# Turning a pair's top-p flags on TensorE behind both tiles' logits, in the second step of a graph attention kernel

## Chip, cores and metric

One core of a Trainium2 chip runs the whole program, in float32 throughout except for some masks. The metric is the device time of one execution in microseconds (us); less is better. TensorE is PE in the profile, its weight loads PEld, VectorE is DVE, ScalarE is ACT, GpSimd is POOL and the DMA queue's engine is SP.

## The reference, cut to what matters

The input is `x`, 3327 rows by 128, and a sparse 3327 x 3327 matrix `adj`. The first layer makes two steps; each of them builds an attention matrix over all rows, keeps in each row only the largest probabilities that together reach 0.9 (top-p), and multiplies. The second layer (signs of `adj`, three heads, gates) follows and is not touched by the change.

```python
def _top_p_attention(X, W1, W2, W3):
    q = X @ W1.T @ W2.T
    k = X @ W3.T
    logits = q @ k.T / TAU
    probs = jax.nn.softmax(logits, axis=-1)
    idx = jnp.argsort(-probs, axis=-1)
    sp = jnp.take_along_axis(probs, idx, axis=-1)
    cs = jnp.cumsum(sp, axis=-1)
    keep_sorted = cs - sp < TOP_P
    ...
    A = probs * mask
    return A / jnp.maximum(A.sum(-1, keepdims=True), 1e-12)
...
for n in range(STEPS):
    A = _top_p_attention(Xa, W1, W2, W3)
    Xf = R @ Xf
    Xa = A @ Xa
    Z = Z + Xf @ U1[n].T + Xa @ U2[n].T
```

`R` is `adj` plus the identity, each row divided by its sum. `X` and `Xa` are 3327 x 128, `q` and `k` 3327 x 64.

## The kernel before

**Tiles and pairs.** The rows are padded to 26 tiles of 128, worked on as 13 pairs, 0 to 12. A tile's logits are 3327 columns wide: seven chunks of up to 512 (`NC`), for which there are two PSUM banks (`lg`), copied by ACT into the tile's row buffer `e`. There are two sets of `e`, so the logits of pair p + 2 go where pair p was, once pair p has been attended. The function `layer0` holds both steps; five engine programs stand side by side in it, each with a fixed order, tied by semaphores.

**Step two (`step == 1`), the part that changes.** Attention runs for the 13 pairs, and between them TensorE does the two products with `adj` (`rows`): 26 units of one pair of tiles in two hops, each unit two tiles of 1 + 26 matmuls. One turn of each engine, for pair p, in program order:

- TensorE (`pair_with_rows`, L992): `take_rows` (L875) gathers the rows that pair p could not settle; `attend` (L944) for the two tiles turns `e` and multiplies it with the features, the first waiting for `select` of tile 0 of pair p and the second for that of tile 1; then `logits(p + 2, 0)`, `turn_flags(p + 1)`, `logits(p + 2, 1)` (L825 and L857); then a chain of small turns and products that go back and forth with ACT (`update_all_rows` L986, `turn_attended` L948, `update` L955); then `rows` (L829) for four tiles.
- VectorE (`pair_with_rows`, L1372), already one pair further while TensorE works on pair p: `search(p + 1)` (L1303) finds the thresholds and ends with `flags_ready`; `tops` (L1285) of the two tiles of pair p + 2 reads their logits in segments of 64 (L71), each waiting for that tile's seven copied chunks by `lg_free`; `assign_slots(p + 1)` (L1314) waits for `flagT_ready`, the turned flags; then it waits for POOL's marks, and `select` (L1346) of the tiles of pair p + 1 lets TensorE attend them (`w_ready`).
- ACT (L1206) copies out what TensorE leaves in PSUM, and takes the exponentials of pair p + 2 (`exps_of`) between the copies of the `rows` tiles.
- POOL (L751): the queries of pair p + 2 (`give_q`), in the first half the scaling of the rows, then `find_marks(p + 1)` (L740), which waits for the same flags as TensorE, then the sums into `H` (`add_rows` L726, `give_attended` L701).

**Turning the flags** (`turn_flags`, L857) is two transposes of one column each (L861) and two products with four columns that count slots (L863 and L864), into the bank `small`. It waits until VectorE's search of that pair is over:

```python
eng.wait_ge(flags_ready, turn_of(step, p) + 1)
eng.wait_ge(rowA_ready, seq(step, p, 0) + 1)
```

**The loops.** `over_pairs_with_rows` (L640) rolls TensorE's pairs 0 to 3 and 7 to 10 in loops of two pairs and writes out pairs 4, 5, 6, 11 and 12; on VectorE 0 to 5 and 7 to 10 are rolled. Pair 6 has one unit of rows to update, the others two. Logits and flags ahead exist for pairs 0 to 10 (`rest >= 2`); for pair 11 only flags.

Of the kernel before, what the change touches and what calls it, by code (L numbers as in the profile page):

```python
# [518 lines left out]
def layer0(nc, d, dims, H, ident):  # L519
# [15 lines left out]
    with ExitStack() as ctx:  # L535
# [77 lines left out]
        def turn_of(step, p):  # L613
            return p + step * PAIRS
# [12 lines left out]
        def at(p, n):  # L627
            return isinstance(p, int) and p == n

        def units_of(p, hop):  # L630

            if at(p, TURN):
                return [(PAIRS - 1, 0)]
            if hop == 0:
                return [(p * 2, 0), (p * 2 + 1, 1)]
            return [(p * 2 - 1, 1), (p * 2, 0)]
# [19 lines left out]
        with nc.Block() as block:  # L656
# [137 lines left out]
            def _(eng):  # L794
# [6 lines left out]
                for step in range(2):  # L801
# [9 lines left out]
                    def logit(p, k, c):  # L811
                        if c == 0 and at(p, PAIRS):
                            eng.wait_ge(taken_q_ready, 1)
                        elif c == 0:
                            eng.wait_ge(qs_ready, seq(step, p, k) + 1)
                        bank = chunk(step, 0, k, c) % 2
                        sl = cols(c, N)
                        eng.wait_ge(lg_free, chunk(step, p, k, c) + 1)
                        eng.matmul(lg[bank][:, 0:sl.stop - sl.start], qs[k][:, :], kT[:, sl],  # L819
                                   start=True, stop=True).then_inc(lg_ready, 1)  # L820
                        if c == NC - 1:
                            eng.drain()
                            eng.sem_inc(qs_free, 1)

                    def logits(p, k):  # L825
                        for c in range(NC):
                            logit(p, k, c)

                    def rows(u, hop):  # L829

                        xf = XR[0] if hop == 0 else XR[2]
                        for k in range(2):
                            eng.wait_ge(adj_loaded[k], (u + 1) * 16)
                            eng.wait_ge(accR_read, u * 2 + k + 1)
                            eng.matmul(accR[:, :], ident[:, :],
                                       xf[:, bass.ds((u - hop * PAIRS) * 2 + k, 1), :].rearrange("p a n -> p (a n)"),
                                       start=True, stop=False)
                            for j in range(T):
                                mm = eng.matmul(accR[:, :], adj[k][:, j * P:(j + 1) * P], xf[:, j, :],  # L839
                                                start=False, stop=(j == T - 1))  # L840
                            mm.then_inc(accR_ready, 1)
                            eng.drain()
                            eng.sem_inc(adj_free, 1)
# [13 lines left out]
                    def turn_flags(p):  # L857
                        eng.wait_ge(flags_ready, turn_of(step, p) + 1)
                        eng.wait_ge(rowA_ready, seq(step, p, 0) + 1)
                        for k in range(1 if at(p, PAIRS) else 2):  # L860
                            mm = eng.transpose(flagT[:, k, :], find.flags[:, k:k + 1], ident[:, :])  # L861
                        if step == 1 and not at(p, PAIRS):
                            eng.matmul(slots, ones, find.counts[:, 1, :], start=True, stop=False)  # L863
                            mm = eng.matmul(slots, upto, find.counts[:, 0, :], start=False, stop=True)  # L864
                        mm.then_inc(flagT_ready, 1)
# [9 lines left out]
                    def take_rows(p):  # L875

                        eng.wait_ge(slots_ready, p + 1)
                        for k in range(2):
                            mm = eng.matmul(taken, hot[k],
                                            XR[1][:, bass.ds(p * 2 + k, 1), :].rearrange("p a n -> p (a n)"),  # L880
                                            start=False, stop=at(p, PAIRS - 1) and k == 1)
                        mm.then_inc(taken_ready, 1)

                    def project_taken():

                        eng.wait_ge(taken_copied, 1)
                        eng.wait_ge(zsA_ready, turn_of(step, PAIRS - 1) + 1)
                        eng.wait_ge(zsR_ready, LATE[0][0])
                        eng.transpose(xt[:, 0, :], taken_rows[:, 0:P], ident[:, :]).then_inc(taken_turned, 1)
                        eng.wait_ge(taken_T_ready, 1)  # L890
                        eng.matmul(zp[0:DA, 0, :], W1T[:, :], taken_T, start=True, stop=True).then_inc(taken_h1_made, 1)
                        eng.wait_ge(taken_h1_ready, 1)
                        eng.matmul(zp[0:DA, 1, :], W2T[:, :], taken_h1, start=True, stop=True).then_inc(taken_q_made, 1)
# [50 lines left out]
                    def attend(p, b, k):  # L944
                        for c in range(NC + 1):
                            attend_part(p, b, k, c)

                    def turn_attended(p):  # L948
                        eng.wait_ge(rowA_ready, seq(step, p, 1) + 2)
                        eng.wait_ge(zsA_ready, turn_of(step, p) + 1)  # L950
                        for k in range(2):
                            mm = eng.transpose(xt[:, k, :], rowA[k][:, :], ident[:, :])
                        mm.then_inc(xtA_ready, 1)

                    def update(p):  # L955
                        eng.wait_ge(xTA_ready, turn_of(step, p) + 1)
                        for k in range(2):
                            mm = eng.matmul(zp[:, k, :], xT[:, k, :], UT[:, 1, step, :], start=True, stop=True)
                        mm.then_inc(zA_ready, 1)
# [26 lines left out]
                    def update_all_rows(units, hop):  # L986
                        for u, s in units:
                            eng.wait_ge(zsR_ready, u)
                            turn_rows(u, s)
                            update_rows(u, hop)  # L990

                    def pair_with_rows(p, b, rest, hop, next_hop):  # L992
                        take_rows(p)
                        if at(p, PAIRS - 1):
                            project_taken()
                            logits(PAIRS, 0)
                        attend(p, b, 0)
                        attend(p, b, 1)
                        if rest >= 2:
                            logits(p + 2, 0)  # L1000
                        if rest:
                            turn_flags(p + 1)
                        if rest >= 2:
                            logits(p + 2, 1)
                        eng.wait_ge(zsA_ready, turn_of(step, p) + 1)
                        if rest:
                            update_all_rows(units_of(p, hop), hop)
                            eng.wait_ge(zsR_ready, units_of(p, hop)[-1][0] + 1)
                        turn_attended(p)
                        update(p)  # L1010
                        if next_hop == 1:
                            eng.wait_ge(hop_done, PAIRS + 2)
                        if next_hop is not None:
                            for u, s in units_of(p + 1, next_hop):
                                rows(u, next_hop)
# [27 lines left out]
                    if step == 0:  # L1043
                        turn_flags(0)
                        over_pairs(eng, pair, tail=3)
                    else:
                        for u, s in units_of(0, 0):
                            rows(u, 0)
                        turn_flags(0)
                        over_pairs_with_rows(eng, pair_with_rows)  # L1050
                        late_rows()
                        turn_flags(PAIRS)
                        attend(PAIRS, 1, 0)
                        update_taken()
                        place_taken()
# [1287 lines left out]
```

## Time and profile before

| what | value |
|---|---|
| runs (3) | 2786.88, 2792.64, 2792.99 us; median 2792.64 us |
| the profiled execution's own time | 2795.35 us |
| its span (first to last instruction) | 2793.6 us |
| step two's attention with rows | about 577 us to 1490 us of the span |
| mean granted TensorE clock | 0.932 of full |
| busy: PE, PEld, DVE, ACT, POOL | 84%, 71%, 79%, 38%, 5% of the span |
| DMA | 245 MB, mean 88 GB/s |

How to read the rows further down: in a list of waits, a row says which engine and line waited for which other engine and line, the us in total, how often, and the longest. In a timeline, a row is the start in us from the span's start, how long in us, engine, line, operation, output<-inputs, how many instructions were merged, and in brackets the idle time just ahead of it and what ended it; "issue" means that the profile shows no releaser.

### The profile page before, as it was taken

The page shows a single profiled execution, that of the slowest core. Times are in us where ns is not written, and L with a number is a line of the kernel's source. Part 1 is how long each engine was busy: PE and PEld are TensorE (multiplying, and loading weights), DVE is VectorE, ACT ScalarE, POOL GpSimd, SP SyncE. Part 2 cuts the span into 40 slices and gives each one's busy share as a digit, 9 for nine tenths or more (in the row PEclk, how much of TensorE's full clock was granted, in tenths as well). Part 3 has the DMA queues.
Part 4 walks back from the last instruction along what each step waited for, and adds up shares of the span by engine and source line. Part 5 has one row for each costly group of instructions (what it writes and reads, how often), then busy time and mean ns, then how long its engine had stood idle before and what let it go on. Part 6 is the DMA issues. An engine that isn't in the chain of part 4 may idle for free. (4 is left out here: it accounts for less than half of the span.)

```text
span 2793.6 us, 53551 instructions
## 1 busy us (share of the span) xinstructions
PE 2358.4 (84%) x17759; PEld 1987.9 (71%) x17759; DVE 2201.9 (79%) x6636; ACT 1071.5 (38%) x1785; POOL 140.9 (5%) x353
## 2 busy tenths in 40 slices
PE   5899998767888997887886649996999999999985
PEld 1566666445677776776775539995999999999952
DVE  3777777288887889888789867775999999999846
ACT  4566666432333333332333040003434344443423
POOL 0000000101111111000000010000000000000000
PEclk9999999988898998998997869998999999999997
DMA  3000000020222221222220234543333333333320
GB/s 127 2 2 1 1 1 2 1 99 11 90 100 100 99 100 50 100 99 100 99 99 2 99 127 175 217 171 126 111 115 133 116 130 118 129 120 126 99 87 25
DMA packets 57106, 245.00 MB, mean 88 GB/s; under 512 B 6705, under 2 KB 18352, under 8 KB 43120
## 3 DMA queue, kind: packets, MB, share of 16 engines
q1 hardware_dynamic: 56816, 241.94, 24.7%
q8 instruction: 83, 1.36, 0.2%
q14 instruction: 207, 1.70, 0.2%
HBM read 235.10 MB, written 6.82 MB: 87 GB/s over the span
## 5 line engine op out<-in xcount | busy, mean ns | idle before, releaser
L1933 PE MATMUL a_acc<-H,pT 128*128 128x128 f32 x4056 | 548.0, 277 | 11.1 <-ACT a_rows L1965 3.8
L1933 PEld LDWEIGHTS a_acc<-H,pT 128*128 128x128 f32 x4056 | 495.4, 192 | 28.1 <-DVE pT L2067 19.3
L71 DVE MAX8 cand<-e 128x8 f32<-128x64 f32 (+3 forms) x1898 | 302.6, 239 | 129.4 <-issue 129.2
L935 PE MATMUL small<-XR,wT 128*128 128x128 f32 x2756 | 377.2, 283 | 28.8 <-ACT wT L1132 28.1
L819 PE MATMUL lg<-kT,qs 128*128 128x512 f32 (+1 forms) x742 | 350.8, 612 | 47.1 <-ACT e L1076 34.9
L935 PEld LDWEIGHTS small<-XR,wT 128*128 128x128 f32 x2756 | 343.1, 197 | 45.1 <-ACT wT L1132 45.1
L2067 DVE TENSOR_TENSOR pT<-a_tr,a_adjT 128x512 f32<-128x512 f32 (+1 forms) x546 | 316.6, 645 | 22.3 <-PE a_tr L1892 19.2
L839 PE MATMUL accR<-XR,adj 128*128 128x129 f32 x2704 | 322.8, 281 | 0.0
L1892 PE MATMUL a_tr<-ident,prob 128*128 128x128 f32 x2028 | 311.9, 274 | 10.9 <-ACTq L1959 10.9
L839 PEld LDWEIGHTS accR<-XR,adj 128*128 128x128 f32 x2704 | 319.5, 198 | 0.0
L1132 ACT ACTIVATE wT<-tr 128x512 f32<-128x512 f32 (+1 forms) x371 | 206.0, 566 | 268.3 <-PE tr L925 266.4
L2045 DVE CUSTOM_DVE_ANT_0 prob<-a_adj,EB 128x3328 f32<-128x3328 f32 x78 | 282.6, 3623 | 0.0
L819 PEld LDWEIGHTS lg<-kT,qs 128*128 128x128 f32 x742 | 124.4, 200 | 215.3 <-ACT e L1076 161.8
L1076 ACT ACTIVATE e<-lg 128x512 f32<-128x512 f32 (+1 forms) x371 | 206.1, 566 | 178.7 <-PE lg L819 176.8
L925 PE MATMUL tr<-ident,e 128*128 128x128 f32 x1378 | 214.0, 283 | 47.9 <-DVE scalars L1353 41.7
L1892 PEld LDWEIGHTS a_tr<-ident,prob 128*128 128x128 f32 x2028 | 241.7, 142 | 11.1 <-issue 11.1
L1957 ACT ACTIVATE prob<-prob,a_negmax 128x3328 f32<-128x3328 f32 x78 | 238.9, 3063 | 9.1 <-DVE a_negmax L2054 9.1
L925 PEld LDWEIGHTS tr<-ident,e 128*128 128x128 f32 x1378 | 168.4, 146 | 87.6 <-issue 44.3
L1581 PE MATMUL g_sp<-g_adj,H 128*128 128x128 f32 x1352 | 162.6, 283 | 17.1 <-ACTq L1646 17.1
L1581 PEld LDWEIGHTS g_sp<-g_adj,H 128*128 128x128 f32 x1352 | 158.5, 198 | 18.8 <-issue 18.2
L1086 ACT ACTIVATE e<-e,scalars 128x3327 f32<-128x3327 f32 x53 | 162.1, 3060 | 15.9 <-DVE scalars L1417 8.8
L219 DVE SCALAR_TENSOR_TENSOR work<-cand,mid 128x416 f32<-128x416 f32 (+1 forms) x198 | 143.3, 758 | 8.1
(334 smaller groups left out, 2456.6 us busy)
## 6 DMA issues: line engine op xcount, KB each, us to landing
adj<-in_adjT SPq DMA_DIRECT2D x52, 1664.0 KB, 7.2
g_adj<-in_adjT SPq DMA_DIRECT2D x26, 1664.0 KB, 6.9
a_adj<-in_adj SPq DMA_DIRECT2D x26, 1664.0 KB, 6.8
a_adjT<-in_adjT SPq DMA_DIRECT2D x156, 256.0 KB, 3.9
a_adjT<-in_adjT SPq DMA_DIRECT2D x26, 128.0 KB, 4.2
XT<-in_x_t SPq DMA_DIRECT2D x1, 1664.0 KB, 13.5
hT_scratch<-hT SPq DMA_DIRECT2D x1, 1664.0 KB, 12.1
nsT_scratch<-nsT SPq DMA_DIRECT2D x1, 1664.0 KB, 6.2
```

Source lines behind the costliest of these rows:

```text
L71: eng.max(cand[:, n, :], src[:, n * seg:min((n + 1) * seg, width)])
L819: eng.matmul(lg[bank][:, 0:sl.stop - sl.start], qs[k][:, :], kT[:, sl], start=True, stop=True).then_inc(lg_ready, 1)
L839: mm = eng.matmul(accR[:, :], adj[k][:, j * P:(j + 1) * P], xf[:, j, :], start=False, stop=(j == T - 1))
L925: mm = eng.transpose(tr[(k * NC + c) % 2][:, o:o + P], e[b][k][:, j * P:(j + 1) * P], ident[:, :])
L935: mm = eng.matmul(accA[:, :], wT[(k * NC + c - 1) % 2][:, o:o + P], xa[:, j, 0:P], start=(j == 0), stop=(j == T - 1))
L1076: eng.activation(e[b][k][:, sl], lg[chunk(step, 0, k, c) % 2][:, 0:sl.stop - sl.start], ACT.Copy).then_inc(lg_free, 1)
L1581: mm = eng.matmul(sp[k][:, :], H[:, j, :], adj[q][:, j * P:(j + 1) * P], start=(j == 0), stop=(j == T - 1))
L1892: mm = eng.transpose(tr[g % BANKS][:, (j % 4) * P:(j % 4 + 1) * P], prob[order[n][1]][:, j * P:(j + 1) * P], ident[:, :])
L1933: mm = eng.matmul(acc[:, :], pT[g % RING][:, (j % 4) * P:(j % 4 + 1) * P], H[:, j, :], start=(j == 0), stop=(j == T - 1))
L1957: eng.activation(prob[h][:, :], prob[h][:, :], ACT.Exp, bias=negmax[h][:, :], accum_out=den[h][:, :])
L2045: eng.tensor_tensor_reduce(prob[h][:, :], adj[k][:, :], EB[:, h, :], 1.0, -3.0e38, ALU.add, ALU.max, mx[h][:, :])
L2067: eng.tensor_tensor(pT[g % RING][:, 0:width(c)], tr[g % BANKS][:, 0:width(c)], adjT[:, c * 512:c * 512 + width(c)], ALU.mult).then_inc(pT_ ...
```

## The change

In TensorE's program for step two, `turn_flags(p + 1)` is written behind `logits(p + 2, 1)`. Nothing is added or removed, and no other engine's program is touched. Step one, whose TensorE program has its own `pair`, stays as it was.

```diff
@@ -998,10 +998,9 @@
                         attend(p, b, 1)
                         if rest >= 2:
                             logits(p + 2, 0)
+                            logits(p + 2, 1)
                         if rest:
                             turn_flags(p + 1)
-                        if rest >= 2:
-                            logits(p + 2, 1)
                         eng.wait_ge(zsA_ready, turn_of(step, p) + 1)
                         if rest:
                             update_all_rows(units_of(p, hop), hop)
```

**Place 1.** TensorE, the rolled pairs of step two, from the end of `logits(p + 2, 0)`. L819 are the logits, L861 to L864 the flags' turn, L859 the wait for the flags, L818 with `l0_qs_ready` that for the next tile's queries. Before:

```order
L819 MATMUL lg<-kT,qs 128x512 [waits l0_lg_free]
L818 REGISTER_ALU
L819 MATMUL lg<-kT,qs 128x255 [waits l0_lg_free]
L859 ISA [waits l0_flags_ready]
L861 MATMUL small<-ident,pair_flags 1x128 [waits l0_rowA_ready]
L861 MATMUL small<-ident,pair_flags 1x128
L863 MATMUL small<-counts,XT 128x4
L864 MATMUL small<-counts,XT 128x4
L815 REGISTER_ALU
L818 ISA [waits l0_qs_ready]
L819 MATMUL lg<-kT,qs 128x512 [waits l0_lg_free]
```

The same place in the changed kernel:

```order
L819 MATMUL lg<-kT,qs 128x512 [waits l0_lg_free]
L818 REGISTER_ALU
L819 MATMUL lg<-kT,qs 128x255 [waits l0_lg_free]
L815 REGISTER_ALU
L818 ISA [waits l0_qs_ready]
L819 MATMUL lg<-kT,qs 128x512 [waits l0_lg_free]
```

The wait for the flags and the four kinds of flag matmuls are gone from between the tiles; the second tile's first chunk follows the first tile's last.

**Place 2.** TensorE, a few instructions on, at the end of `logits(p + 2, 1)`; L846 and L848 begin the chain of small updates. Before:

```order
L819 MATMUL lg<-kT,qs 128x512 [waits l0_lg_free]
L818 REGISTER_ALU
L819 MATMUL lg<-kT,qs 128x255 [waits l0_lg_free]
L846 ISA [waits l0_zsR_ready,l0_zsA_ready]
L848 MATMUL xz<-ident,rawR 128x128 [waits l0_rowR_ready]
```

In the changed kernel:

```order
L819 MATMUL lg<-kT,qs 128x512 [waits l0_lg_free]
L818 REGISTER_ALU
L819 MATMUL lg<-kT,qs 128x255 [waits l0_lg_free]
L859 ISA [waits l0_flags_ready]
L861 MATMUL small<-ident,pair_flags 1x128 [waits l0_rowA_ready]
L861 MATMUL small<-ident,pair_flags 1x128
L863 MATMUL small<-counts,XT 128x4
L864 MATMUL small<-counts,XT 128x4
L846 ISA [waits l0_zsR_ready,l0_zsA_ready]
L848 MATMUL xz<-ident,rawR 128x128 [waits l0_rowR_ready]
```

The wait for the flags now stands ahead of the updates and of the rows behind them, and no longer ahead of logits.

**Place 3.** VectorE, the end of a search and what follows it, which is the same in both kernels: `tops` of two tiles, each behind the copied logits (`l0_lg_free`), then `assign_slots` at L1318 behind the turned flags.

```order
L1288 ISA
L1290 MEMSET gate 128x1 [waits l0_lg_free]
L71 MAX cand<-e 128x8 x52
L1293 TENSOR_REDUCE scalars<-cand 128x1
L1295 TENSOR_SCALAR scalars<-scalars 128x1
L1288 ISA
L1290 MEMSET gate 128x1 [waits l0_lg_free]
L71 MAX cand<-e 128x8 x52
L1293 TENSOR_REDUCE scalars<-cand 128x1
L1295 TENSOR_SCALAR scalars<-scalars 128x1
L1318 TENSOR_REDUCE pair_flag_top<-small 1x2 [waits l0_flagT_ready]
```

Nothing moved here; what moves are the times at which the second wait for `l0_lg_free` and the wait for `l0_flagT_ready` are met.

## Rows read from the trace of the kernel before

**Rows 1.** The waits of VectorE, then of TensorE, 576 to 1500 us.
```profile
DVE cand L71 <- issue: 34.9, 11, 9.6
...
PE small L861 <- DVEq L326: 46.1, 8, 9.6
```
**Rows 2.** Timeline of TensorE in pair 2, a pair without a wait for flags.
```profile
826.70 0.38 PE L861 MATMUL small<-ident,pair_flags 128*1 128x128 f32 x2 [0.25 <-issue]
...
827.28 6.12 PE L819 MATMUL lg<-kT,qs 128*128 128x512 f32 x14
833.75 0.43 PE L848 MATMUL xz<-ident,rawR 128*128 128x128 f32 x2 [0.35 <-issue]
...
838.71 0.66 PE L952 MATMUL xz<-ident,rowA 128*128 128x128 f32 x2 [0.66 <-ACT zsR L1125]
```
**Rows 3.** Timeline of TensorE in pair 1, which waits for the flags of pair 2.
```profile
748.36 0.59 PE L861 MATMUL small<-ident,pair_flags 128*1 128x128 f32 x2 [5.84 <-DVEq L326]
...
749.45 8.66 PE L819 MATMUL lg<-kT,qs 128*128 128x512 f32 x14
758.37 0.41 PE L848 MATMUL xz<-ident,rawR 128*128 128x128 f32 x2 [0.26 <-issue]
```
**Rows 4.** Timeline of VectorE: its idle times ahead of `tops`, searches 1 to 5 and 7 to 10.
```profile
680.58 0.22 DVE L71 MAX8 cand<-e 128x8 f32<-128x64 f32 x1 [2.48 <-issue]
...
758.58 0.22 DVE L71 MAX8 cand<-e 128x8 f32<-128x64 f32 x1 [2.81 <-issue]
...
826.91 0.22 DVE L71 MAX8 cand<-e 128x8 f32<-128x64 f32 x1 [7.07 <-issue]
...
912.04 0.22 DVE L71 MAX8 cand<-e 128x8 f32<-128x64 f32 x1 [2.95 <-issue]
...
974.10 0.22 DVE L71 MAX8 cand<-e 128x8 f32<-128x64 f32 x1 [0.86 <-issue]
...
1121.46 0.22 DVE L71 MAX8 cand<-e 128x8 f32<-128x64 f32 x1 [1.95 <-issue]
...
1193.45 0.22 DVE L71 MAX8 cand<-e 128x8 f32<-128x64 f32 x1 [1.73 <-issue]
...
1271.17 0.22 DVE L71 MAX8 cand<-e 128x8 f32<-128x64 f32 x1 [2.31 <-issue]
...
1341.34 0.22 DVE L71 MAX8 cand<-e 128x8 f32<-128x64 f32 x1 [9.61 <-issue]
```
**Rows 5.** Timeline of TensorE in pairs 6, 7 and 8: flags' turn and start of updates.
```profile
1112.09 0.59 PE L861 MATMUL small<-ident,pair_flags 128*1 128x128 f32 x2 [7.85 <-DVEq L326]
...
1121.24 0.41 PE L848 MATMUL xz<-ident,rawR 128*128 128x128 f32 x2 [0.29 <-issue]
...
1184.39 0.59 PE L861 MATMUL small<-ident,pair_flags 128*1 128x128 f32 x2 [5.36 <-DVEq L326]
...
1193.27 0.43 PE L848 MATMUL xz<-ident,rawR 128*128 128x128 f32 x2 [0.34 <-issue]
...
1261.45 0.59 PE L861 MATMUL small<-ident,pair_flags 128*1 128x128 f32 x2 [6.09 <-DVEq L326]
...
1271.12 0.41 PE L848 MATMUL xz<-ident,rawR 128*128 128x128 f32 x2 [0.41 <-issue]
```
**Rows 6.** Timeline of TensorE in pair 11, with updates right behind a wait for flags.
```profile
1479.13 0.59 PE L861 MATMUL small<-ident,pair_flags 128*1 128x128 f32 x2 [5.13 <-DVEq L326]
...
1480.22 0.67 PE L848 MATMUL xz<-ident,rawR 128*128 128x128 f32 x2
...
1485.91 0.69 PE L952 MATMUL xz<-ident,rowA 128*128 128x128 f32 x2 [0.47 <-ACT zsR L1125]
```
**Rows 7.** Timeline of TensorE in pair 2: the first two tiles of `rows`.
```profile
841.29 7.10 PE L839 MATMUL accR<-XR,adj 128*128 128x129 f32 x52
...
849.17 5.97 PE L839 MATMUL accR<-XR,adj 128*128 128x129 f32 x52
```
**Rows 8.** Timeline of VectorE in search 3: the second tile's `tops`.
```profile
834.14 6.68 DVE L71 MAX8 cand<-e 128x8 f32<-128x64 f32 x52
```

## The prediction

> **What bounds the kernel now.** I read the waits of step two first [rows 1]. VectorE sits idle ahead of its `tops` (L71) for 34.9 us in 11 pieces; "issue" names no releaser, but L1290 in front of them waits for copied logits and nothing else. TensorE waits 46.1 us for VectorE's flags in 8 pieces (L861 behind the last drain of the search). So the two engines wait for each other in turns, and both waits meet at the place that the change touches. Then the timelines. In pair 2 [rows 2] the flags are ready when TensorE comes: it goes from flags at 826.70 over the second tile's logits at 827.28 to the updates at 833.75, so a tile's logits take 833.75 - 827.28 = 6.47 us. In pair 1 [rows 3] it waits 5.84 us at the flags; then the logits, 6.12 us in pair 2, take 8.66 us, and from flags to updates it is 758.37 - 748.36 = 10.0 us, of which 749.45 - 748.36 = 1.1 us are the flags' turn. VectorE, which has just finished the search, reads the first tile at once, but must wait for the second (2.81 us at 758.58) [rows 4]. These logits depend on nothing of the search: they stand behind the flags by program order alone.
>
> **The change part by part.** No instruction and no DMA is added or removed; two matters move.
>
> *The flags' turn goes behind the second logits.* Where the flags are ready, it comes 6.5 us later. That costs nothing: VectorE needs it at L1318, after the second tile's `tops`, which starts when the same logits are copied and takes 6.68 us [rows 8], against 0.58 us for the turn (827.28 - 826.70) [rows 2]. If that cover were gone, each pair would pay 0.6 to 1.1 us.
>
> *The second logits go ahead of the wait.* I follow how much earlier each engine gets to its work, pair by pair. VectorE's gain is what it no longer waits. TensorE's gain, where a wait for the flags is left, is VectorE's gain at that search plus the time from flags to updates less the 1.1 us of the turn. A wait of w is left if w, plus TensorE's lead over VectorE, exceeds 6.5 us (a logits' length).
>
> - Searches 1 and 2: VectorE's waits for second tiles go, 2.48 + 2.81 = 5.3 us [rows 4].
> - TensorE, pair 1: it has won some 8.6 us in pair 0 (a whole slow second logits, 8.66 us in [rows 3]), VectorE 2.5; 5.84 + 6.1 - 6.5 = 5.4 us of wait are left, so it gains 2.5 + 10.0 - 1.1 = 11.4 us [rows 3].
> - Search 3 waits 7.07 us for the first logits of pair 4, which TensorE made late. TensorE is now ahead by 11.4 - 5.3 = 6.1 us, so 6.1 of the 7.07 go. Searches 4 and 5: 2.95 and 0.86 go [rows 4]. VectorE has gained 5.3 + 6.1 + 3.8 = 15.2 us. In pairs 2 to 5 TensorE doesn't wait for flags any more and is further ahead than that; in pair 6, with one unit of rows for two, it waits for VectorE's `select`, so its lead is lost and both stand at 15.2 us.
> - Pairs 6, 7 and 8 have waits of 7.85, 5.36 and 6.09 us [rows 5], and a wait is left in each (7.85 - 6.5, and more with the lead in the other two). VectorE gains 1.95 (search 7) and 1.73 us (search 8), so 18.9 us at search 9 [rows 4]. TensorE's gain in pair 8 is 18.9 + (1271.12 - 1261.45) - 1.1 = 18.9 + 8.6 = 27.5 us; by the same sum it had 23.2 in pair 6 and 24.9 in pair 7.
> - Pairs 9 and 10 have no wait for flags; TensorE keeps 27.5 us. VectorE gains 2.31 us more in search 9, to 21.2 us, and its 9.61 us of waiting for first logits in search 10 shrink by the 6.3 us between the two. From there both are 27.5 us early, and pairs 11 and 12, the late rows and the second layer follow unchanged.
>
> *What the wait's new place costs.* Behind it stand now the updates. Pair 11, which has no logits to make, shows that pattern already [rows 6]: after 5.13 us of waiting, L848 to L952 take 1485.91 - 1480.22 = 5.69 us, against 838.71 - 833.75 = 4.96 in pair 2 [rows 2]. So 0.73 us in each pair where a wait is left; two of them count in the sum (pair 1, by way of search 3, and pair 8): 1.5 us. The other end is nothing at all, as the updates run partly at half speed in any pair. POOL's marks (`find_marks`) start with the flags and now meet the updates' sums on POOL's queue; in pair 11 they meet likewise, so that is within the 0.73.
>
> The rows show what a wait costs besides itself: after 5.84 us without work the second logits take 8.66 instead of 6.12 us [rows 2, 3], as their first matmuls run at the lower of the two clock levels, 1.2 GHz. The Trainium skill (TensorE: Matmul & The Clock Gate, HAM oscillation) says that a gap in TensorE's work is paid for again by the matmuls behind it, which start slow. The trace agrees. By that rule alone the moved wait would slow `rows` by what it no longer takes from the logits, 2.5 us in each of the two pairs that count, and the gain would be 27.5 - 5.1 = 22.4 us.
>
> The sum: 27.5 - 1.5 = 26.0 us. The profiled execution took 2795.35 us, 2.7 above the median of the runs, 2792.64; so 2769.3 for its like and 2766.6 for the median. The bounds: VectorE's search, `tops` and `select` have no other wait for TensorE worth naming, so the gain can't exceed the 34.9 us of [rows 1]: 2757.7. Below, it is rival A.
>
> **The rivals.**
>
> A. *The lead is not turned into earlier first logits.* Only the waits for second tiles go, 2.48 + 2.81 + 2.95 + 1.95 + 1.73 + 2.31 = 14.2 us, and the 7.07 and 9.61 us stay, because something else paces TensorE: ACT, which takes exponentials between the `rows` copies, or the transfers of `adj`. Against it: TensorE's rows show it busy between the flags of one pair and the next wherever it isn't waiting for VectorE. 2778.4 us.
>
> B. *Nothing.* The second logits turn out to wait as well, for their queries from POOL, or both engines find a new wait (exponentials that come late for the search) as long as the old one. Against it: POOL gives the queries before it waits for the flags itself. 2792 us.
>
> C. *Slower, by the clock.* TensorE now idles just ahead of the updates, which are too sparse to keep it fast, and then of `rows`. After the updates the first tile of rows took 7.10 us, the next 5.97 [rows 7]; about 1.1 us are lost to the lower level today. If the whole first tile ran at half speed, it would cost 5.97 - 1.13 = 4.8 us more in all 11 pairs, 53 us, against 27.5 gained: 2818 us. It decides from 2.5 us more per pair (27.5 / 11). Against it: pair 11 lost 0.73, and only some five pairs keep a wait. The rule of the Trainium skill named above leans this way, but would find no wait left to act on in pairs 2 to 5, 9 and 10.
>
> D. *More.* The slow stretches after the waits go too, and VectorE loses nearly all its 34.9 us: 2760 us.
>
> **How the numbers follow.** A difference below 0.3% (8.4 us) is about what a measurement of this kernel can't tell from none. Forecast (18 to 31 us gained) 0.67; A 0.14; B 0.08; C 0.04; D 0.07. The predicted time is the forecast's, 2766.6. The range takes in D and the bound, less a little for the spread of the runs, down to 2756, and A with some 4 us above it, up to 2782; B and C are left out, 0.12. Faster: 0.67 + 0.14 + 0.07 = 0.88; same 0.08; slower 0.04.
>
> **What would show it.** In the changed profile: waits of L71 in step two down from 34.9 to 5 to 10 us, with none ahead of second tiles. Waits for flags in TensorE (L861) left in five or six pairs, pairs 0, 1, 6, 7, 8 and 11, at 1 to 6 us, about 20 us in all, and none in pair 3. Second logits at 6.1 us everywhere. L848 to L952 at 5.0 to 5.7 us. L1318 never waiting for pairs 1 to 11. Step one and everything from pair 12 on as long as before. I am wrong if TensorE's lead shows up as longer waits for `select` (tr, L925) of the same size, if the waits at first logits stay at 7 and 9.6 us, or if the tiles of `rows` at the lower level grow by more than one per pair.

## The result, and the profile after

The changed kernel takes 2770.14 us in the median of 4 runs (2768.09 to 2773.17), against 2792.81 us for the kernel before in the same job: 22.7 us less, ratio 0.9918, 95% interval 0.9902 to 0.9933. A second job, with 9 runs of it, gave 0.9927 (0.9909 to 0.9945). The prediction was 2766.6 us, with a range of 2756 to 2782. The profiled execution took 2770.99 us against 2795.35, 24.4 us less.

The page of the changed kernel, its span and the rows of TensorE's logits and `rows` matmuls (busy us, mean ns of one, idle ahead and releaser):

```profile
span 2769.2 us, 53551 instructions
...
L819 PE MATMUL lg<-kT,qs 128*128 128x512 f32 (+1 forms) x742 | 339.9, 596 | 50.5 <-ACT e L1075 38.5
...
L839 PE MATMUL accR<-XR,adj 128*128 128x129 f32 x2704 | 327.2, 283 | 0.0
```

The same two rows of the page before:

```profile
L819 PE MATMUL lg<-kT,qs 128*128 128x512 f32 (+1 forms) x742 | 350.8, 612 | 47.1 <-ACT e L1076 34.9
...
L839 PE MATMUL accR<-XR,adj 128*128 128x129 f32 x2704 | 322.8, 281 | 0.0
```

The same instructions are there. The logits are busy 10.9 us less. Before, six second tiles (pairs 0, 1, 3, 6, 7 and 8) took 7.45 to 8.76 us behind a wait for flags, with a granted clock of 0.50 (1.2 GHz) in their first 2 us; now all second tiles take 6.1 us. The `rows` matmuls are busy 4.4 us more.

VectorE's waits in step two, 576 to 1480 us, in the changed kernel (total, times, longest; lines from L1004 on stand one lower than before):

```profile
DVE work L444 <- issue: 28.2, 17, 2.6
...
DVE gate L1304 <- issue: 10.3, 3, 4.7
DVE e L450 <- issue: 6.0, 4, 2.1
DVE cand L71 <- issue: 4.7, 3, 2.9
```

and those rows before that were not shown yet:

```profile
DVE work L444 <- issue: 24.8, 11, 3.3
DVE gate L1305 <- issue: 12.2, 3, 4.4
...
DVE e L450 <- issue: 2.4, 2, 1.3
```

TensorE's waits in the same stretch, changed kernel:

```profile
PE tr L925 <- DVE scalars L1352: 24.6, 4, 11.6
...
PE small L861 <- DVEq L326: 15.0, 8, 3.1
```

VectorE's waits for logits fall from 34.9 us [rows 1] to 4.7, by 30.2 us, and TensorE's for flags from 46.1 to 15.0; part of that comes back as a longer wait for `select` (L925, 16.9 us before). But VectorE's idle times inside `select`, behind its branches (L444 and L450), rise from 27.2 to 34.2 us. A search starts at L1305, in the changed kernel at L1304. The starts of searches 0, 7 and 12, before:

```profile
576.77 0.06 DVE L1305 MEMSET gate<- 128x1 f32 x1
...
1087.62 0.06 DVE L1305 MEMSET gate<- 128x1 f32 x1
...
1454.83 0.06 DVE L1305 MEMSET gate<- 128x1 f32 x1
```

and in the changed kernel, with what is left of the wait in search 10:

```profile
577.99 0.06 DVE L1304 MEMSET gate<- 128x1 f32 x1
...
1078.42 0.06 DVE L1304 MEMSET gate<- 128x1 f32 x1
...
1317.37 0.22 DVE L71 MAX8 cand<-e 128x8 f32<-128x64 f32 x1 [1.59 <-issue]
...
1429.74 0.06 DVE L1304 MEMSET gate<- 128x1 f32 x1
```

From search 0 to search 12 it took 1454.83 - 576.77 = 878.1 us before and 1429.74 - 577.99 = 851.8 after: 26.3 us less. VectorE's waits add up to nearly that: 30.2 for logits, 1.9 at the turns of the loops, less 7.0 in `select`, is 25.1.

Pair 1 on TensorE, changed kernel, timeline:

```profile
737.58 6.13 PE L819 MATMUL lg<-kT,qs 128*128 128x512 f32 x14 [0.39 <-ACT e L1075]
746.37 0.38 PE L861 MATMUL small<-ident,pair_flags 128*1 128x128 f32 x2 [2.66 <-DVEq L326]
...
746.98 0.67 PE L848 MATMUL xz<-ident,rawR 128*128 128x128 f32 x2
...
752.85 0.66 PE L952 MATMUL xz<-ident,rowA 128*128 128x128 f32 x2 [0.66 <-ACT zsR L1124]
...
755.43 6.81 PE L839 MATMUL accR<-XR,adj 128*128 128x129 f32 x52
```

Against [rows 3]: the second logits take 6.13 us, not 8.66; of the wait 2.66 us are left, not 5.84; the updates begin at 746.98, not 758.37. L848 to L952 take 5.87 us, 0.9 more than in a pair without a wait [rows 2] and 1.3 more than in pair 1 before. The first tile of `rows` takes 6.81 us, against 7.44 in pair 1 before; but in pair 8, which keeps a wait too, it takes 7.78 against 6.93.

### The profile page after: what moved, and what is told of

It reads as the page before. It is cut to its first block and busy times, and to the rows that moved or that the text cites. A ratio compares the mean times of both kernels' runs of the same rounds, so it can differ in the third digit from the quotient of the medians.

```text
span 2769.2 us, 53551 instructions
## 1 busy us (share of the span) xinstructions
PE 2355.1 (85%) x17759; PEld 1987.9 (72%) x17759; DVE 2199.7 (79%) x6636; ACT 1072.5 (39%) x1785; POOL 141.5 (5%) x353
## 5 line engine op out<-in xcount | busy, mean ns | idle before, releaser
L1932 PEld LDWEIGHTS a_acc<-H,pT 128*128 128x128 f32 x4056 | 495.3, 192 | 28.7 <-DVE pT L2066 19.9
L935 PE MATMUL small<-XR,wT 128*128 128x128 f32 x2756 | 375.9, 282 | 28.3 <-ACT wT L1131 27.5
L71 DVE MAX8 cand<-e 128x8 f32<-128x64 f32 (+3 forms) x1898 | 302.7, 240 | 101.4 <-issue 101.2
L819 PE MATMUL lg<-kT,qs 128*128 128x512 f32 (+1 forms) x742 | 339.9, 596 | 50.5 <-ACT e L1075 38.5
L2066 DVE TENSOR_TENSOR pT<-a_tr,a_adjT 128x512 f32<-128x512 f32 (+1 forms) x546 | 316.3, 643 | 22.5 <-PE a_tr L1891 19.3
L1891 PE MATMUL a_tr<-ident,prob 128*128 128x128 f32 x2028 | 311.2, 274 | 10.9 <-ACTq L1958 10.9
L819 PEld LDWEIGHTS lg<-kT,qs 128*128 128x128 f32 x742 | 119.0, 193 | 216.9 <-ACT e L1075 168.6
L925 PE MATMUL tr<-ident,e 128*128 128x128 f32 x1378 | 213.2, 282 | 56.0 <-DVE scalars L1352 49.9
L925 PEld LDWEIGHTS tr<-ident,e 128*128 128x128 f32 x1378 | 167.7, 146 | 95.7 <-DVE scalars L1352 51.6
L1580 PEld LDWEIGHTS g_sp<-g_adj,H 128*128 128x128 f32 x1352 | 161.9, 201 | 18.8 <-issue 18.2
```

The source lines that it names most:

```text
L71: eng.max(cand[:, n, :], src[:, n * seg:min((n + 1) * seg, width)])
L925: mm = eng.transpose(tr[(k * NC + c) % 2][:, o:o + P], e[b][k][:, j * P:(j + 1) * P], ident[:, :])
L935: mm = eng.matmul(accA[:, :], wT[(k * NC + c - 1) % 2][:, o:o + P], xa[:, j, 0:P], start=(j == 0), stop=(j == T - 1))
L1580: mm = eng.matmul(sp[k][:, :], H[:, j, :], adj[q][:, j * P:(j + 1) * P], start=(j == 0), stop=(j == T - 1))
L1891: mm = eng.transpose(tr[g % BANKS][:, (j % 4) * P:(j % 4 + 1) * P], prob[order[n][1]][:, j * P:(j + 1) * P], ident[:, :])
L1932: mm = eng.matmul(acc[:, :], pT[g % RING][:, (j % 4) * P:(j % 4 + 1) * P], H[:, j, :], start=(j == 0), stop=(j == T - 1))
```

## Where the extra time in `select` comes from

Search 9's `select` of tile 0 shows both cases. Before, VectorE and SP:

```profile
1281.89 3.62 DVE L439 MATCH_REPLACE8 work<-hits,e 128x3336 f32<-128x3336 f32 x1
1285.58 0.09 DVE L444 MATCH_VALUE_LOAD work<-drops,work 128x8 f32 x1
...
1285.72 14.26 SPq L673 DMA_DIRECT2D adj<-in_adjT  x3
```

In the changed kernel:

```profile
1263.19 14.26 SPq L673 DMA_DIRECT2D adj<-in_adjT  x3
...
1264.27 3.62 DVE L439 MATCH_REPLACE8 work<-hits,e 128x3336 f32<-128x3336 f32 x1
1269.79 0.09 DVE L444 MATCH_VALUE_LOAD work<-drops,work 128x8 f32 x1 [1.91 <-issue]
```

Between L439 and L444 VectorE branches over the rarely run code of another search round. Before, the first transfer of an `adj` tile (three here, some 7 us each) is issued when that branch is already past; now TensorE is further ahead of VectorE, so the transfer is in flight, and VectorE stands idle for 1.91 us. The DMA view of the stretch 1267.5 to 1269.8 us, changed kernel, and of 1285 to 1285.6 us, before (queue, kind: packets, MB, share of 16 engines):

```profile
q1 hardware_dynamic: 58, 0.56, 58.7%
q8 instruction: 1, 0.02, 2.4%
q14 instruction: 1, 0.01, 0.8%
```
```profile
q14 instruction: 1, 0.01, 4.5%
```

A packet of the instruction queue falls into this place in both; before it had the DMA engines to itself and VectorE did not wait.

The timelines of all pairs show the same shift. In `select` of tile 0 the idle at L444 and L450 rises from 3.1 us (2 pieces) to 17.8 (10), as transfers are now under way there; in that of tile 1 it falls from 24.1 to 16.4, as fewer transfers are left by then. The experiments test what the transfers do to it.

## The experiments

Unless said otherwise an edit is made to the changed kernel. Times are medians, ratios those to the kernel before in the same job, with a 95% interval. The runs up to the flags behind the updates were made in one job with the changed kernel's nine runs. The later ones were made in two other jobs, so "less than the changed kernel" compares medians of different jobs there; the kernel before lay between 2792.81 and 2795.38 us in the four jobs. A list of waits comes from one profiled execution.

### The changed kernel again

> The changed kernel once more, so that the other runs of this job have it on their own chip. Both theories: 22 to 26 us below the kernel before, VectorE's waits at L71 in step two 4 to 8 us in all.

2771.29 us in 9 runs (2767.76 to 2781.42), ratio 0.9927. L71 waited 11.9 us in this execution, more than the 4 to 8 expected: search 3 waited 5.45 us for first logits again, and search 10 3.04. L444 and L450 waited 32.1. Single executions differ by some us in how the two engines fall in.

### The new order in one half of the pairs

```diff
                         if rest >= 2:
                             logits(p + 2, 0)
-                            logits(p + 2, 1)
+                            if hop == 0:
+                                logits(p + 2, 1)
                         if rest:
                             turn_flags(p + 1)
+                        if rest >= 2 and not (hop == 0):
+                            logits(p + 2, 1)
```

> The new order in pairs 0 to 6 alone, the old order in pairs 7 to 10. Theory 1 (the gain is VectorE's waits for logits, which TensorE's wait for the flags held up, added up along the chain of pairs): 15 to 17 us faster than the kernel before, and in pairs 7 to 11 L71 waits again, about 15 to 19 us in all. Rival (the gain is the clock: second logits that run slow behind a wait, 2.5 us each, on TensorE's own path): two of the five slow ones are in pairs 0 and 1, so 5 us faster, and VectorE's waits hardly less.

2784.85 us in 10 runs, ratio 0.9971 (0.9955 to 0.9987), so 9.3 us less by the medians and 8 by the ratio. With `hop == 1` in its place, pairs 7 to 10:

> The old order in pairs 0 to 6, the new one in pairs 7 to 10. Theory 1: 8 to 11 us faster than the kernel before; with the run of the first half it adds up to the whole, 24 to 28. Rival (one half frees the path for both): either run alone gives 20 or more, and the sum is well above the whole.

2783.22 us in 10 runs, ratio 0.9971 (0.9957 to 0.9984), 10.9 us less by the medians and 8 by the ratio. VectorE's waits in the first and in the second run:

```profile
DVE work L444 <- issue: 28.0, 16, 3.1
DVE cand L71 <- issue: 21.1, 7, 9.4
```
```profile
DVE cand L71 <- issue: 23.8, 14, 6.6
DVE work L444 <- issue: 19.6, 10, 2.9
```

The second half does what theory 1 said; the first half gives 8 to 9 us, not 15 to 17. Its waits for logits fall by 13.8 us, near the forecast, but a third of that is lost at L444 and L450 (31.6 us against 27.2). Together the two give 16 us by the ratios and 20 by the medians, where the whole gives 20 to 23: not well above it (the rival of the second run falls), and within the intervals not clearly below it, but less than the 24 to 28 of theory 1. The clock rival fails on the waits: it had them hardly less, and in the first half they fell by 13.8 us.

### Flags one step later, behind the updates

```diff
                             logits(p + 2, 0)
                             logits(p + 2, 1)
-                        if rest:
-                            turn_flags(p + 1)
 ...
                         turn_attended(p)
                         update(p)
+                        if rest:
+                            turn_flags(p + 1)
```

> The changed kernel with the flags' turn moved on by one more step, behind the updates and just ahead of the rows. Theory 1: of the 15 us that TensorE still waits for flags nearly all go, but VectorE is what bounds now and has 5 us left to win: 0 to 5 us faster than the changed kernel. Rival (the cover is gone: VectorE's assign_slots, L1317 and after, now waits for the flags' turn, which comes about 8 us after the second logits where tops takes 7): 0.5 to 1 us at L1317 or so in each of 11 pairs, 5 to 11 us slower than the changed kernel.

2781.81 us in 10 runs, ratio 0.9946 (0.9926 to 0.9966): 10.5 us slower than the changed kernel in that job. The size is the rival's; its reason, that the cover is gone, holds in pair 11 alone. In the other pairs something shows that neither had. Timeline near 750 us:

```profile
746.71 0.20 POOL L744 TENSOR_TENSOR pool_gate<-scalars 128x1 f32<-128x1 f32 x1 [23.85 <-DVEq L326]
...
751.15 0.72 POOL L730 TENSOR_TENSOR H<-H,zsR 128x256 f32 x1 [0.35 <-issue]
752.02 0.38 ACT L1124 ACTIVATE zsR<-xz 128x256 f32<-128x256 f32 x1 [4.84 <-POOLq L731]
...
752.64 0.66 PE L952 MATMUL xz<-ident,rowA 128*128 128x128 f32 x2 [4.19 <-ACT zsR L1124]
```

POOL waits for the flags in `find_marks` (L744), and its sums (L730) stand behind that. ACT's copy of the second unit's update needs the first sum, and TensorE's L952 needs the copy. So TensorE waits for the flags by another way: L952 waited 31.9 us in all. And in pair 11, which has no logits, VectorE has no `tops` to cover the turn:

```profile
1467.81 0.41 DVE L1317 TENSOR_REDUCE pair_flag_top<-small 1x2 f32<-1x256 f32 x1 [9.53 <-PE small L864]
```

The starts of the searches tell what each of the two costs. Search 12 of this run:

```profile
1434.07 0.06 DVE L1304 MEMSET gate<- 128x1 f32 x1
```

With search 0 at 578.13 that is 855.9 us for the twelve pairs. The changed kernel took 851.8 in its first profile and 858.1 in the second, so the way by POOL costs no time that shows there, but theory 1's gain isn't there either. From search 12 to the end of the span it takes 1348.7 us, against 1339.5 and 1336.2. So most of the 10.5 us lies behind search 12, where pair 11's wait stands.

To take both away, POOL's marks go behind its sums, and pair 11 stays as in the changed kernel:

```diff
-                            find_marks(p + 1)
+                            if rest == 1:
+                                find_marks(p + 1)
                             for u, s in units_of(p, hop):
                                 add_rows(u, hop)
                             give_attended(p)
+                            if rest >= 2:
+                                find_marks(p + 1)
 ...
```

In TensorE's program `turn_flags` stands behind the updates for `rest >= 2` and where the changed kernel has it for `rest == 1`.

> The run with the flags behind the updates again, with two edits: POOL's find_marks stands behind add_rows and give_attended, and pair 11, which has no logits, keeps flags and marks where the changed kernel has them. Theory (behind updates, TensorE waited for the flags all the same: the second unit's copy on ACT waits for POOL's add_rows, which stands behind find_marks, which waits for the flags; and pair 11 cost VectorE 8 us at L1317): TensorE's waits at L952 fall from 31.9 us to about 9 and no wait of 9.5 us is left at L1317; 8 to 15 us faster than the run behind updates, and 0 to 5 faster than the changed kernel, as VectorE bounds. Rival (TensorE's own late turn holds up VectorE's assign_slots in every pair): waits at L1317 of 5 us or more in all, and no faster than the changed kernel.

2766.75 us in 4 runs, ratio 0.9910 (0.9881 to 0.9938); the runs lie between 2759.04 and 2772.45, and the profiled one is the fastest. VectorE's wait for the turned flags, TensorE's for `select`, at L952 (L955 here) and for the flags:

```profile
DVE pair_flag_top L1322 <- PE small L867: 4.2, 2, 2.9
```
```profile
PE tr L928 <- DVE scalars L1357: 33.4, 9, 12.4
...
PE xz L955 <- ACT zsR L1129: 7.2, 12, 0.7
...
PE small L864 <- DVEq L326: 5.7, 1, 5.7
```

With both mended the loss is gone, and the later turn is as fast as the changed kernel, not measurably faster. Both edits were made in one run, so it doesn't tell them apart; the search starts above put most of the loss on pair 11. TensorE's waits for flags are nearly gone and stand at `select` instead (33.4 us): VectorE bounds.

### Transfers of `adj` cut short

After the first two, each transfer in step two brings 128 of 3328 columns, so these runs leave out most of the loading of `adj` there and multiply with old columns.

```diff
 ...
-                            eng.dma_start(adj[k][:, :], d["adjT"][bass.ds((q * 2 + k) * P, P), :]).then_inc(adj_loaded[k], 16)
+                            eng.dma_start(adj[k][:, 0:P], d["adjT"][bass.ds((q * 2 + k) * P, P), 0:P]).then_inc(adj_loaded[k], 16)
```

> The changed kernel with each transfer of adj in step two, but the first two, cut from 3328 to 128 columns; the products with adj then use the first two tiles' columns over and over, so the rows of R are not the reference's. 
2751.31 us in 4 runs, ratio 0.9848 (0.9822 to 0.9873): 20 us less than the changed kernel. VectorE's waits:

```profile
DVE cand L71 <- issue: 19.9, 5, 7.1
...
DVE gate L1308 <- issue: 9.2, 3, 3.1
```

L444 and L450 are not in the list at all any more: 34 us of idle time gone, with the same branches and nearly the same number of instruction packets (158 in queues q8 and q14 from 560 to 1480 us, against 156 in the changed kernel). So the branch alone costs nothing that shows, and the transfers make the stall. At the loops' turns most of the idle stays. VectorE being faster, it waits for TensorE again (L71 19.9 us). The 20 us are not the stalls' price alone: TensorE's own waits for `adj`, 7.8 us in the changed kernel, are gone too.

> The kernel before with the same cut of the transfers of adj, the rows of R again not the reference's. Theory (the transfers cost the new order more than the old, since tile 0's select now falls into them too): the new order gains more without them, so this run is 28 to 34 us slower than the changed kernel with the same cut. Rival (the transfers have no part in what the change gave): it is slower by 22 to 26 us, as with whole transfers.

2763.87 us in 4 runs, ratio 0.9890 (0.9865 to 0.9915): the change is worth 12.6 us there, below both expectations. Its L71 waits 32.7 us, so only 12.8 less with the new order. A reading that fits, but was not tested apart: without its stalls VectorE's searches end earlier, TensorE waits for flags 28.0 us, not 46.1, and a change that takes logits from behind that wait has less to give. What the theory wanted, a larger gain once the stalls in `select` are gone, did not come.

### Less code to jump over, and no loops

```diff
             with eng.If(eng.snap(kind) > OPEN - 1):
                 eng.drain()
-                with eng.Fori(0, 3):
-                    with eng.If(eng.snap(flag) > OPEN - 1):
-                        another()
                 while_over(eng, flag, OPEN - 1, self.width // 8, another)
```

> The changed kernel with the rarely run code of another search round standing once instead of twice in each select (its loop of three is left out, the nested loop behind it does the same work), so the branch in select jumps over half the code. Theory (the stall is a fetch of the code behind the jump): the shorter jump needs the fetch less often or earlier, and the idle at L444 and L450 falls from 34 us by a third or more, 5 to 15 us faster than the changed kernel. Rival (what counts is that a branch is taken at all): within 3 us of it.

2764.81 us in 4 runs, ratio 0.9897 (0.9875 to 0.9919); 6 us below the changed kernel. L444 waits 23.6 us, and L450 is not in the list any more, against 34.2 for the two: 10.6 less, just under the third that was expected. The time is at the lower end of what was expected, and its interval overlaps that of the changed kernel, so by the time alone it is not told apart from it.

```diff
 ...
+            if unroll:
+                for p in range(PAIRS):
+                    hop = 0 if p <= TURN else 1
+                    rest = min(3, PAIRS - 1 - p)
+                    nxt = None if p >= PAIRS - 2 else (1 if p >= TURN else 0)
+                    pair(p, p % 2, 3 if rest >= 2 else rest, hop, nxt)
+                return
 ...
```

TensorE's and VectorE's programs of step two call it with `unroll=True`.

> The changed kernel with the pairs of step two written out on TensorE and VectorE in place of loops. Theory: the idle at the turns of the loops, 10 us on VectorE (L1304, three times) and about 5 us twice on TensorE, goes; VectorE bounds, so 6 to 10 us faster than the changed kernel. Rival (longer code makes the fetches at the branches in select later or more): as fast or slower, with L444 above 30 us.

2756.66 us in 4 runs, ratio 0.9862 (0.9842 to 0.9883): 14 us less, more than expected, although L444 waits more:

```profile
DVE work L444 <- issue: 35.7, 20, 2.9
```

The turns of the loops are gone from the list (10.3 us on VectorE), and TensorE has lost its own two. L450 waits 1.9 us instead of 6.0, L71 0.3 instead of 4.7. With the 7.5 us more at L444 that makes 11.3 of the 14.

Both edits together:

> The written-out pairs and the single copy of the round code together, in the new order. Theory (each takes other stalls of VectorE away): the gains add, 14 + 6 = 20 us below the changed kernel, about 2750. Rival (TensorE takes over as the bound once VectorE has fewer stalls): 14 to 16 us, with L71's waits above 10 us.

2738.57 us in 4 runs, ratio 0.9800 (0.9774 to 0.9827): 57 us below the kernel before in its job (2795.38) and 32 below the changed one. It beats both theories. VectorE's waits:

```profile
DVE work L444 <- issue: 10.3, 7, 2.2
...
DVE cand L71 <- issue: 7.1, 3, 3.4
```

The waits of VectorE at L444, L450, the loops' turns and L71 make up 29.6 us of that. The two gains don't just add (6 + 14): in straight code with the shorter jump only 7 branches stall, against 20 with the longer one. Why the jump's length matters so much more there is open.

> The same, with the flags' turn back between the two tiles. Theory (what the change is worth hangs on how much VectorE lags: with its stalls of adj gone it was worth 12.6 us, and with the loops' stalls gone it lies between): 12 to 22 us slower than the same kernel in the new order. Rival (the order is worth the same everywhere): 22 to 26.

2760.59 us in 4 runs, ratio 0.9876 (0.9848 to 0.9903): the change is worth 22.0 us in this kernel, at the border between the two expectations, so this run does not tell them apart. L71 waits 22.5 us there, 15.4 more than in the new order, and L444 18.2 us, 7.9 more. So here the new order has less idle at the branches, not more as in the kernel with loops.

> Written out, single copy, flags behind the updates and POOL's marks behind its sums. Theory (with a quicker VectorE the 15 to 20 us that TensorE waits for flags begin to count): 2 to 8 us faster than the same without the last two moves. Rival (VectorE still bounds): within 2 us of it, with L71's waits below 5 us.

2746.54 us in 4 runs, ratio 0.9825 (0.9795 to 0.9856): 8 us slower than without the last two moves by the medians, though the intervals of the two ratios overlap. The theory falls. The rival's reason holds, L71 below 5 us as VectorE still bounds, but not its "within 2 us":

```profile
DVE work L444 <- issue: 16.4, 11, 2.7
...
DVE e L450 <- issue: 4.0, 3, 2.1
...
DVE cand L71 <- issue: 2.5, 1, 2.5
```

L71 falls by 4.6 us, L444 and L450 rise from 12.5 to 20.4. That is 3.3 us net, near the 4.1 us between the two profiled executions, and less than the 8 between the medians. It fits what the change did in the kernel with loops, where a freer TensorE moved its transfers into VectorE's branches; the run before this one went the other way, so it is no rule.

## Why the prediction was right

**The mechanism** was the forecast one. Second logits no longer wait for the flags, VectorE no longer waits for second logits, and first logits come earlier since TensorE's lead is carried over: search 3 waited 7.07 us [rows 4] and doesn't any more, search 10's 9.61 us are 1.59. (In the second profile of the changed kernel 5.45 and 3.04 us were left.) Rival A, which kept both whole, falls; B and C fall with the time. D was half right: VectorE lost nearly all its waits, 30.2 of 34.9 us. Most of the 4.7 us left, 2.89, is a wait in search 11 for first logits, which was 2.86 us before and stands in no term of the sum.

**The sum, part by part.** *VectorE's waits*: forecast 34.9 down to 5 to 10 us, found 4.7. *TensorE's waits for flags*: about 20 us forecast, 15.0 found; pairs 4 and 5, forecast to have none, wait 1.29 and 1.57 us. *The second logits at 6.1 us everywhere*: found. *The flags' later turn at no cost*: nothing new at L1317, 4.2 us in 2 waits against 4.4 in 2 before; that cover is gone in pair 11, as the run behind the updates showed, but the change does not touch that pair. *The price of 1.5 us behind the moved wait*: it is there, but it did not reach the end. Pair 1 paid 1.3 us in L848 to L952 (5.87 against 4.55 before), and search 3 had no wait left that it could lengthen. Pair 8 paid 0.6 in L848 to L952 (5.46 against 4.86) and 0.85 in the first tile of `rows`; yet TensorE's first logits of pair 9 came 1334.75 - 1310.77 = 24.0 us earlier, as its updates in pair 8 had (1271.12 - 1247.14), so both were made up in between, where the granted clock over the first 4.6 us of pair 9's work was 0.64, against 0.50 before. The Trainium skill's rule (TensorE: Matmul & The Clock Gate, HAM oscillation) would have left 22.4 us of gain by the prediction's working, close to the measured 22.7, but not for its reason. The trace agrees with it in pair 8 and not in pair 1, where the first tile of `rows` was 0.6 us faster than before, and what was paid in pair 8 didn't last.

**The step that was missing.** "VectorE's search, `tops` and `select` have no other wait for TensorE worth naming" holds, but they are held up by what TensorE sets off. Transfers of `adj` start when TensorE ends a tile of `rows`; now they overlap `select` of tile 0 as well. In VectorE's list of waits 7.0 us of 30.2 go back there. That is how this execution adds up, not a price that can be taken off: with the transfers cut short the change gave 12.6 us and not more, and in the written-out kernel with the short jump the new order had less idle at L444.

**What was luck.** The forecast's 27.5 came from letting all of VectorE's own times stand. Counted from search 0, VectorE was 12.5 us early at search 4 (forecast 11.4), then only 10.4 at search 7 (15.2) and 17.2 at search 10 (21.2). There TensorE's lead was 8.0 us and not 6.3, so search 10 gave more than forecast, and at search 11 VectorE was 25.5 us early (27.5). So the sum came out near by two errors of opposite sign. Within step two the profiled executions differ by 26.3 us, within the whole by 24.4 (search 0 started 1.2 us later in the changed kernel) and the medians by 22.7, against 26.0 predicted; the last 2 to 4 us are within what single executions differ by.

## What to carry to other kernels

When one engine's instruction waits for a result, look what stands behind it in program order without needing that result, and who waits for it; the gain is the sum along the chain of both engines, until one of them bounds alone. Before moving a wait further, follow every other queue that waits for the same event: here POOL and ACT brought it back by another way, and in the one pair without logits the waiting engine had nothing to fill the time. And when a freed engine starts large transfers earlier, see whether the other engine's branches fall into them; whether that costs or gives time changed from one kernel to the next here.

## What the runs showed of the hardware that was not expected

- VectorE's branch over a large block of code costs nothing that shows while no large transfer is in flight, and up to 2.6 us (28.2 us in 17 stalls in the changed kernel) while 1664 KB transfers are, with 8 to 16 KB instruction packets in the same place; with 64 KB transfers all these stalls vanished.
- Turns of the loops cost 2.8 to 4.7 us each on VectorE (10.3 us in 3), and 9.2 us in 3 were left with short transfers, so these are for the most part not the transfers' doing.
- Writing 13 pairs out in straight code and halving the block jumped over took 32 us off a 2770 us kernel, with the same arithmetic.
